# A macaron block on one core: silu written over the gate product, routing of row pairs in the bank set free, one norm shift and three last-row additions moved

## What is computed

```python
x = x + 0.5 * _L0_ffn_ref(_layernorm(x, axis=-1), ...)
x = x + _L0_attn_ref(_layernorm(x, axis=-1), ...)
x = x + 0.5 * _L0_ffn_ref(_layernorm(x, axis=-1), ...)
```

```python
h = jnp.einsum('td,edf->etf', x, gate_w)
u = jnp.einsum('td,edf->etf', x, up_w)
y = jnp.einsum('etf,efd->etd', jax.nn.silu(h) * u, down_w)
routed = jnp.einsum('etd,te->td', y, combine)
sh = jax.nn.silu(x @ sh_gate_w) * (x @ sh_up_w) @ sh_down_w
```

## Time and profile before

| | us |
|---|---|
| median of 3 runs (906.88 to 907.73) | 907.09 |
| the profiled execution | 906.35 |
| its span, first to last instruction | 904.6 |
| TensorE busy (share of the span) | 866.9 (96%) |
| VectorE busy | 729.0 (81%) |
| GpSimd busy | 651.1 (72%) |
| ScalarE busy | 541.4 (60%) |
| mean granted TensorE clock, share of full | 0.992 |

### The profile page before, as it was taken

The page is one execution under the profiler, slowest core; times in us unless marked ns, Lnnn a source line. Parts: engine busy times, 40 slices in busy tenths (PEclk is TensorE's granted clock), DMA queues, the critical chain, the costliest instruction groups (busy, mean ns, idle before and its releaser), DMA issues. The chain is left out here.

```text
span 904.6 us, 12232 instructions
## 1 busy us (share of the span) xinstructions
PE 866.9 (96%) x3591; PEld 622.5 (69%) x3591; DVE 729.0 (81%) x1255; ACT 541.4 (60%) x951; POOL 651.1 (72%) x480
## 2 busy tenths in 40 slices
PE   8999999999999798999999997899999999999997
PEld 7777788887767575455455544477777788788885
DVE  4989868877975478999999999887987787796664
ACT  7565565565555477668676684356556556555554
POOL 7758776776755467998899896756677677676765
PEclk9999999999999899999999998999999999999999
DMA  8715374363344142444444343341537536545440
GB/s 206 223 50 162 116 213 120 118 151 129 95 137 110 59 141 94 153 151 142 140 163 157 127 156 125 101 145 55 169 91 199 160 125 155 152 117 161 148 126 23
DMA packets 120611, 121.34 MB, mean 134 GB/s; under 512 B 55000, under 2 KB 78688, under 8 KB 120544
## 3 DMA queue, kind: packets, MB, share of 16 engines
q1 hardware_dynamic: 102352, 116.35, 42.2%
q10 hardware_dynamic: 18192, 4.21, 2.2%
HBM read 111.87 MB, written 8.65 MB: 133 GB/s over the span
## 5 line engine op out<-in xcount | busy, mean ns | idle before, releaser
L721 POOL TENSOR_TENSOR act_lo<-act,act_hi 128x512 fp32r<-128x512 f32 x288 | 372.0, 1296 | 208.6 <-ACT act_hi L834 208.4
L827 ACT ACTIVATE bank<-bank 128x512 f32<-128x512 f32 x252 | 146.6, 582 | 239.3 <-PE bank L1162 212.7
L1158 PE MATMUL bank<-x_parts,w_hi 128*128 128x512 f32 x572 | 233.2, 408 | 15.1 <-DVE act L1036 12.5
L1058 DVE TENSOR_TENSOR sg<-bank,c_ring 128x512 f32<-128x512 f32 x252 | 172.1, 683 | 92.9 <-ACT bank L827 85.5
L1036 DVE SCALAR_TENSOR_TENSOR act<-sg,bank 128x512 f32<-128x512 f32 x288 | 197.8, 687 | 35.4 <-PE bank L1162 22.6
L1162 PE MATMUL bank<-x_parts,w_hi 128*128 128x512 f32 x572 | 226.0, 395 | 0.0
L1159 PE MATMUL bank<-x_parts,w_lo 128*128 128x512 f32 x572 | 225.9, 395 | 0.0
L834 ACT ACTIVATE act_hi<-act 128x512 fp32r<-128x512 f32 x288 | 179.2, 623 | 1.1 <-PE bank L1134 0.8
L1158 PEld LDWEIGHTS bank<-x_parts,w_hi 128*128 128x128 f32 x572 | 107.7, 188 | 53.2 <-DVE act L1036 22.3
L1162 PEld LDWEIGHTS bank<-x_parts,w_hi 128*128 128x128 f32 x572 | 107.7, 188 | 25.6
L1159 PEld LDWEIGHTS bank<-x_parts,w_lo 128*128 128x128 f32 x572 | 107.8, 189 | 24.8 <-issue 1.7
(11 more groups left out here) (182 smaller groups left out, 992.7 us busy)
## 6 DMA issues: line engine op xcount, KB each, us to landing
c_ring<-c_dram SPq DMA_DIRECT2D x252, 256.0 KB, 3.7
c_ring<-c_dram SPq DMA_DIRECT2D x64, 512.0 KB, 3.6
y_dram<-out_t SPq DMA_DIRECT2D x56, 64.0 KB, 2.9
y_tok<-y_dram SPq DMA_DIRECT2D x14, 256.0 KB, 3.6
xt_dram<-xn ACTq DMA_DIRECT2D x32, 64.0 KB, 3.4
xt<-xt_dram ACTq DMA_DIRECT2D x8, 256.0 KB, 3.0
out<-x_sb SPq DMA_DIRECT2D x7, 256.0 KB, 2.3
x_sb<-in_L_attn_hidden_states SPq DMA_DIRECT2D x3, 512.0 KB, 5.9
```

Of the source, the lines that this page charges most:

```text
L721: self.nc.gpsimd.tensor_tensor(m["act_lo"][:, g % LAG], m["act"][:, g % ACTS], m["act_hi"][:, g % LAG].bitcast(FP32), ALU.subtract).then_i ...
L827: nc.scalar.activation(self.s_bank[:, g % 2], self.h_bank[:, g % 2], ACT.Silu).then_inc(self.sg_ready, 1)
L1058: nc.vector.tensor_tensor(m["sg"][:, g % 2], silu, weight, ALU.mult).then_inc(self.w_done, 1)
L1158: nc.tensor.matmul(dst, m["w_hi"][:, k, n, :], x_hi, start=True, stop=False)
```

## The change

- **Silu in place.** Silu g is written over the gate product, in h_bank[g % 2], and VectorE reads it there. ScalarE's waits for w_done and for Mamba's last reads go away. Gate g on TensorE waits for w_done of g-2 (sg_ready where the silu goes to SBUF), by pe_wait_gate_bank. TensorE's wait for the last w stands before Mamba's first spread.
- **Routing in a bank.** s_bank is free, and its second half takes what scratch took for row 0 (route_bank): for all row pairs of both feed-forwards and for row 1 of f2. Row 1 of f1 stays in SBUF. A routing in a bank has 27 steps.
- **Late shift.** Entry 121 of HEAD_DVE becomes 125.
- **Last row.** The additions of ADDED are left out in Mamba's row 7; TensorE sums both halves there.

```diff
--- before.py
+++ after.py
@@ -111,7 +111,7 @@
         score_rows = sb("score_rows", [P, 2, P])
-        score = sb("score", [P, 2 * TT, Q])
+        score = sb("score", [P, TT, Q])
         biased = sb("biased", [P, 2 * TT, E])
...
@@ -263,7 +263,7 @@
-HEAD_DVE = (101, 102, 104, 106, 107, 109, 110, 120, 121, 134, 140)
+HEAD_DVE = (101, 102, 104, 106, 107, 109, 110, 120, 125, 134, 140)
 HEAD_POOL = (102, 107, 120, 126)
...
@@ -566,7 +566,8 @@
-    FIRST_STEPS, ROUTE_STEPS = 27, 25
...
+    ROUTE_STEPS, LESS = 27, 2
     STORED = 16 * P // Q
...
@@ -606,14 +607,20 @@
+    def route_bank(self, r):
...
+        if r == 0:
+            return self.scratch
+        return None if self.p == 0 and r == 1 else self.s_bank[:, 1]
...
     def route_score(self, r, rows):
...
-        nt = rows * TT
-        if r == 0:
-            return self.scratch[:, 0:nt * Q].rearrange("p (t e) -> p t e", t=nt)
-        return self.m["score"][:, TT * (r % 2):TT * (r % 2) + nt]
+        nt, bank = rows * TT, self.route_bank(r)
+        if bank is not None:
+            return bank[:, 0:nt * Q].rearrange("p (t e) -> p t e", t=nt)
+        return self.m["score"][:, 0:nt]
...
@@ -819,12 +826,7 @@
                 else:
-                    if self.mamba and g == NSH:
-                        ae.wait_ge(self.mamba.y_ready, BATCH)
-                    if self.mamba and g == NSH + 1:
-                        ae.wait_ge(self.mamba.x_added, BATCH)
-                    need(ae, self.w_done, i * E + k - NSH - 1)
-                    nc.scalar.activation(self.s_bank[:, g % 2], self.h_bank[:, g % 2], ACT.Silu
+                    nc.scalar.activation(self.h_bank[:, g % 2], self.h_bank[:, g % 2], ACT.Silu
                                          ).then_inc(self.sg_ready, 1)
...
@@ -867,7 +869,8 @@
         tiles = slice(TT * (r % 2), TT * (r % 2) + nt)
-        s = Steps(dve, self.route_step, self.FIRST_STEPS + (b - 1) * self.ROUTE_STEPS if b else 0)
+        bank = self.route_bank(r)
+        s = Steps(dve, self.route_step, b * self.ROUTE_STEPS - (self.LESS if self.p == 0 and b > 1 else 0))
         (biased, pair_sum, g_score, g_ge, g_gt, masked, top8, above, tied, n_above, tie_at, picked, total) = (
...
@@ -875,12 +878,12 @@
         g_rank = g_rank.rearrange("p (t g) -> p t g", t=nt)
-        if r == 0:
-            part = lambda n: self.scratch[:, n * nt * E:(n + 1) * nt * E].rearrange("p (t e) -> p t e", t=nt)
+        if bank is not None:
+            part = lambda n: bank[:, n * nt * E:(n + 1) * nt * E].rearrange("p (t e) -> p t e", t=nt)
             biased_too = masked = weighted = part(2)
...
             tied = part(3)
-            total_too = self.scratch[:, 3 * nt * E:3 * nt * E + nt]
+            total_too = bank[:, 3 * nt * E:3 * nt * E + nt]
             g_score_too = g_rank = turned[:, :, E:E + GROUPS]
...
@@ -972,7 +975,7 @@
                                        ALU.mult, ALU.mult).then_inc(self.comb_ready, 1)
-        assert s.n == (self.ROUTE_STEPS if r else self.FIRST_STEPS), s.n
+        assert s.n == self.ROUTE_STEPS - (self.LESS if bank is None else 0), s.n
         yield
...
@@ -1047,7 +1050,7 @@
                     dve.wait_ge(self.sg_ready, g + 1)
-                    silu, weight = self.s_bank[:, g % 2], m["c_ring"][:, e % C_SLOTS, :]
+                    silu, weight = self.h_bank[:, g % 2], m["c_ring"][:, e % C_SLOTS, :]
                     if self.p == 0 and w < SPREAD:
...
@@ -1176,6 +1179,15 @@
+    def pe_wait_gate_bank(self, pe, j):
...
+        if j >= 0:
+            i, k = divmod(j, NE)
+            if k < NSH or self.p == 0 and j < NSH + SPREAD:
+                pe.wait_ge(self.sg_ready, j + 1)
+            else:
+                pe.wait_ge(self.w_done, i * E + k - NSH + 1)
...
     def pe_first_blocks(self, pe):
...
@@ -1215,7 +1227,7 @@
                     pe.wait_ge(self.mamba.scan_done, ALL_PAIRS - 1)
-                need(pe, self.sg_ready, g - 1)
+                self.pe_wait_gate_bank(pe, g - 2)
                 self.pe_product(pe, self.h_bank[:, g % 2], 0, g).then_inc(self.h_ready, 1)
...
@@ -1342,7 +1354,7 @@
                 product = nc.gpsimd.tensor_tensor(state, state, m["c_ring"][:, 2 * (n % RING):2 * (n % RING) + 2], ALU.mult)
-                if n in ADDED:
+                if n in ADDED and i < BATCH - 1:
                     product.then_inc(self.weighted, 1)
...
@@ -1634,7 +1646,7 @@
         pe.wait_ge(self.mul_done, g + 1)
-        for s in range(1 if n in ADDED else 2):
+        for s in range(1 if n in ADDED and i < BATCH - 1 else 2):
             last = self.nc.tensor.matmul(self.y_acc, self.m["ident"][:, :], self.state(g)[:, s, :], start=False,
...
@@ -1684,12 +1696,11 @@
         pe.wait_ge(self.setup.selector_done, 1)
-        pe.wait_ge(f1.sg_ready, BLOCKS)
+        pe.wait_ge(f1.w_done, BATCH * E)
         self.pe_spread(pe, 0)
...
         pe.wait_ge(f1.act_ready, BLOCKS)
-        pe.wait_ge(f1.w_done, BATCH * E)
         self.norm.pe_transpose(pe, BATCH + 2, self.misc)
...
```

## The result

The kernel after takes 894.91 us in the median of 4 runs (893.89 to 895.35), beside 906.99 for the kernel before on the same chip; ratio 0.9864, 95% interval 0.9847 to 0.9881, so 10.8 to 13.9 us less. Forecast were 895.5, in a range of 893.0 to 900.0. In a later set of runs it took 895.14 (ratio 0.9856, 0.9840 to 0.9872). The total is right; of its four terms two were mis-sized, in opposite directions.

The account below looks back on a forecast made before the run. TensorE, busy 96% of the span, was taken as the bound, its idle time as winnable. 7.0 + 4.3 + 0.3 = 11.6 us off the profiled 906.35 gave 894.75, as a median 895.5; range 893.0 to 900.0.

Parts of the forecast that it names:

- The head, 7.0: Late shift, end of first feed-forward: block 124's up product comes 5.0 us earlier, and full clock behind it wins 2.0.
- the clock: TensorE's half clock from 302.22 to 306.20, after 5.33 us idle, was to become full clock: 2.0 us won.
- The margin at GpSimd: GpSimd's low part of block 121 was to end just when its down product asks: margin 0, 0 to 0.5 us given back.
- Routing in a bank, 4.3: Routing in both feed-forwards: faster VectorE operations remove TensorE's stops, 4.3 us won, bounds 0 and 5.
- the step that counted only the stops visible in rows 12: Five TensorE stops beside routing in the profile before, 0.47 to 1.10 us idle each; 3.8 us of them counted as won.
- Silu in place, 0: Feed-forward blocks: gate waits one product earlier but up starts as before; silu stays 0.58 us; net 0.
- Last row, 0.3: Mamba's last row: without GpSimd's additions its last product and the waiting sum start earlier, gain 0.3 us, from 0 to 0.3.
- 1: Rival: the head keeps its clock loss or gains a new wait at GpSimd's queue, 898.0 us; chance 0.12.
- 2: Rival: the bank makes routing no faster or the two added operations eat the gain, 899.8 us; chance 0.10.
- 3: Rival: the late shift fails, VectorE or ScalarE being held there by something else, 902.5 us; chance 0.05.
- 5: Rival: no change, 2 and 3 together; chance 0.03.
- 4: Rival: slower, the in-place silu at 1.55 us binds the blocks, 17.6 us lost, 913; chance 0.03.

Follow-up runs that it names:

- the two kernels: Kernel before with only the shift moved behind act of block 125: 901.08 us; kernel after with the shift back behind block 121: 901.82 us.
- the two kernels that undo one part: Kernel after with pair and f2 row 1 routing back in SBUF: 903.02 us; kernel after with the shift back behind block 121: 901.82 us.
- The filler: Kernel before plus 20 extra TensorE products in front of block 124's up product, keeping TensorE at work during the wait: 906.17 us, ratio 0.9986.

## Why the prediction was right, point by point

- **The head, 7.0: right in mechanism, place and size.** 6.84 by trace, 6.5 and 6.2 to 6.9 by the two kernels. The wait was 5.03 of it (forecast 5.0), the clock 1.8 (forecast 2.0). The margin at GpSimd was 0.4 us at down(121), not 0; what its full queue held was act(124) on VectorE, by 1.94 us, which the forecast doesn't name and which cost nothing at TensorE.
- **Routing in a bank, 4.3: mechanism right, size too small.** Taking it out of the kernel after costs 7.3 to 8.1. What failed is the step that counted only the stops visible in rows 12, as if the other parts of the change left the routing alone. In the kernel with the silu in place there are more of them (0.35 and 0.12 at block 26, 0.07 at block 24 of f2) and the operations are stretched more (15.3 us of VectorE beside 14.2). Against the kernel before the bank wins 5.7 by trace, before the silu's cost. The places were right: every one of rows 12 is gone. The reason given, "stretched by a GpSimd operation", was argued then and is shown now for rows 2 and 3 of f1.
- **Silu in place, 0: wrong by +1.6 us (0.6 to 2.6).** The duration is right, 582 ns. The argument "gate starts when w(g-2) ends, up when it did before" holds at the stops. It failed where I named only g = 19: where w(g-2) or silu(g-2) ends between the due times of gate and up the gate is late and the up was not, and that happened at g = 16 too, 0.34 us, while g = 19 cost 0.37 with nothing swallowed. These are gates that wait where no up had waited, which the prediction names as a sign of being wrong. And it did not see that shifted blocks meet GpSimd at other operations, nor that a gate behind a long stop runs at half clock.
- **Last row, 0.3: direction right, 0.16 by one execution.** It is below what the time can tell.
- The two errors cancel, and that is luck: 4.3 + 0 forecast, about 5.7 - 1.6 by the trace of the kernel after. By the times, the bank taken out of the kernel after and the silu put into the kernel before, it is 7.3 to 8.1 less 1.6. So the two together are worth 4.1 to 6.5 us, and each alone depends on the other. A right total does not show that the terms are right.
- **Rivals.** 1 falls by the windows at 1.00. 2 and 3 by the two kernels that undo one part, and 5 with them. 4 by the silu's 582 ns. Against the skill's figure the prediction set the bank's 0.23 us alone; without the same operation in SBUF that doesn't decide it. Now it can be decided. For the same 128x128 scalar-tensor operation the runs show 0.30 us with a bank and 0.29 in SBUF beside GpSimd's short operations. The fixed 120 cycles against 58 that the Trainium skill (VectorE: DVE Perf Modes, section on the TRN2 errata) gives a PSUM source would be an estimated 0.065 us; the trace has 0.01.

## What to carry to other kernels

Small VectorE operations on two SBUF operands beside a busy GpSimd can take as long as GpSimd's operation (here 0.29 us became up to 1.39); look for min and max of one line, and if they differ fourfold, try an operand in a bank. A wait that is moved to an earlier product of the same queue is free only where both would have stopped; list the blocks where the awaited end falls between the two due times. When a stop is removed by moving one entry of an order, ask who else is queued for that entry: here it was ScalarE, and the stop moved one block on.

## What was not expected of the hardware

How long ScalarE stands at a DMA issue varies between executions. In each stretch of stores it makes eight issues, and there are four stretches in each of the thirteen profiled executions. Six of the eight take 0.58 to 0.88 us each; the fifth takes 0.58 to 1.83 and the last 0.65 to 1.70. A block leaves ScalarE 0.9 us (2.10 less 0.58 and 0.62), so four in a row put it 1.7 us or more behind.

Whether TensorE notices goes by the sum of the second four. With four in a row, TensorE doesn't wait at blocks 48 to 50 and 84 to 86 in any of the 30 stretches where they take up to 3.09 us. Of the four stretches from 3.15 to 3.24 two show 0.03 and 0.04 us, and all ten from 3.25 on show a wait of 0.08 to 0.87. The longest wait is in the kernel with the routing in SBUF, whose second four took 4.09 us. Timeline of ScalarE's issues and TensorE there, at block 49 of f2:

```profile
685.79 1.83 ACTq L753 DMA_DIRECT2D xt_dram<-xn  x1
...
691.37 0.50 PE L1161 MATMUL bank<-x_parts,w_hi 128*128 128x512 f32 x1 [0.87 <-DVE sg L1061]
```

The filler's 0.48 (3.71 us) and the 0.23 of the silu alone (3.46 us) at this block are of the same kind. So these stops belong to the issues and not to the part under test, and in the profile of the kernel before the four never took more than 2.78 us: a comparison by trace with it puts the stops of the others on the change. That goes for 0.9 us of the 1.6 lost by the kernel after, at its two blocks 85. In pairs the issues no longer stopped TensorE, even where the second four took 3.51 us in sum; that is one such stretch, and the other seven are too short to tell. Why the fifth and the last vary isn't shown.
